# A fused attention kernel's gate split into two calendar steps, with a rearranged calendar

## The reference

```python
# cross attention on 77 context rows, 16 heads of 32, keys masked by length
x = x + softmax(mask((LN(x) @ Wq) @ (ctx @ Wk).T / sqrt(32))) @ (ctx @ Wv) @ Wo

# self attention whose four projections are mixtures of low-rank experts
y = LN(x)
h = relu(mean(y, axis=tokens) @ gw1.T + gb1)          # the gate: one vector a sample
logits = h @ gw2.T + gb2                              # 8 experts
top_vals, top_idx = top_k(logits, 2)
gates = softmax(top_vals)
# for p in q, k, v, o:
#   p(y) = y @ Wm.T + sum_k gates[k] * ((y @ V[idx_k].T) * S[idx_k]) @ U[idx_k].T + b
x = x + o(softmax(q(y) * scale @ k(y).T) @ v(y))
```

## Time and profile before

| | us |
|---|---|
| median of 3 runs | 1512.65 |
| lowest and highest | 1509.66, 1518.13 |
| the profiled execution | 1515.14 |
| its span, first to last instruction | 1513.4 |

### The profile page before, as it was taken

The page is one execution under the profiler, slowest core; times in us unless marked ns, Lnnn a source line. Parts: engine busy times, 40 slices in busy tenths (PEclk is TensorE's granted clock), DMA queues, the critical chain, the costliest instruction groups (busy, mean ns, idle before and its releaser), DMA issues.

```text
span 1513.4 us, 17021 instructions
## 1 busy us (share of the span) xinstructions
PE 1415.1 (94%) x5624; PEld 704.1 (47%) x5624; DVE 987.9 (65%) x1719; ACT 860.1 (57%) x1491; POOL 680.9 (45%) x411
## 2 busy tenths in 40 slices
PE   4998999899989999899989999899989999899877
PEld 3534444455444454445444454455445444444332
DVE  4363577776777677776777677776777676665552
ACT  1425374866467664766557664776557664655441
POOL 2011125454645354454545354354545354556553
PEclk9878999999999999999999999999999999899977
DMA  5423322522324322622334222522234221521220
GB/s 203 111 94 103 78 57 74 153 68 61 99 80 107 80 54 81 165 60 71 81 98 106 76 58 78 157 71 71 75 104 105 75 60 50 154 56 36 56 61 28
DMA packets 78238, 130.80 MB, mean 86 GB/s; under 512 B 26358, under 2 KB 31094, under 8 KB 75079
## 3 DMA queue, kind: packets, MB, share of 16 engines
q1 hardware_dynamic: 74055, 128.66, 31.9%
q10 hardware_dynamic: 4096, 1.06, 0.3%
HBM read 66.08 MB, written 12.21 MB: 52 GB/s over the span
## 4 chain that ended last, share of the span: by engine, by line
PE 82%; ACT 5%; DMA 4%; DVE 4%; SPq 3%; issue 2%; POOL 1%; ACTq 0%; POOLq 0%; DVEq 0%
PE pj L1090 40%; PE sc L1147 8%; PE acc L1204 8%; PE scT L1175 8%; PE sc L1136 3%; PE pj L1084 2%; PE scT L1168 2%; PE pj L1192 2%; PE pj L1120 2%; PE pj L1184 2%; DMA qsc<-qsc 2%; PE pj L1213 2%; ACT probs L816 2%; SPq L581 1%; PE pj L1076 1%
## 5 line engine op out<-in xcount | busy, mean ns | idle before, releaser
L816 ACT ACTIVATE probs<-scT 128x512 f32<-128x512 f32 x512 | 290.4, 594 | 320.2 <-PE scT L1175 317.8
L928 DVE TENSOR_REDUCE negmax<-sc 128x1 f32<-128x512 f32 x512 | 338.3, 684 | 156.7 <-PE sc L1147 155.2
L1147 PE MATMUL sc<-ks,qs 96*128 96x512 f32 x512 | 295.0, 599 | 35.5 <-DVE negmax L928 27.6
L679 POOL TENSOR_TENSOR probs_sum<-probs_sum,probs 128x1024 f32<-128x1024 f32 x128 | 300.7, 2366 | 58.1 <-ACT probs L816 57.6
L955 DVE RECIPROCAL inv_sum<-pj 128x128 f32<-128x128 f32 x256 | 224.1, 920 | 63.3 <-PE pj L1192 27.9
L1175 PE MATMUL scT<-qs,ks 99*128 99x512 f32 x512 | 250.6, 523 | 8.6 <-ACT probs L816 4.5
L1090 PE MATMUL pj<-XT,Wqk 128*128 128x512 f32 x512 | 257.7, 605 | 0.3 <-DVE Wqk L1027 0.2
L675 POOL TENSOR_TENSOR probs_sum<-probs 128x1024 f32<-128x1024 f32 x64 | 150.8, 2369 | 179.8 <-ACT probs L816 179.7
L685 POOL TENSOR_TENSOR uv_stack<-UVS_sb,uv_stack 96x1024 fp32r<-96x1024 f32 x32 | 75.6, 2361 | 246.9 <-ACT UVS_sb L723 246.9
L1147 PEld LDWEIGHTS sc<-ks,qs 96*128 96x128 f32 x512 | 100.6, 198 | 141.0 <-issue 75.0
L1175 PEld LDWEIGHTS scT<-qs,ks 99*128 99x128 f32 x512 | 98.4, 196 | 128.7 <-ACT probs L816 61.4
(11 more groups left out here) (102 smaller groups left out, 1753.7 us busy)
## 6 DMA issues: line engine op xcount, KB each, us to landing
Wqk<-in_WmT SPq DMA_DIRECT2D x16, 1024.0 KB, 5.9
Wvo<-in_WmT SPq DMA_DIRECT2D x16, 1024.0 KB, 7.5
UVS_sb<-in_UVS SPq DMA_DIRECT2D x64, 192.8 KB, 3.5
qs<-stage_lo SPq DMA_DIRECT2D x136, 64.0 KB, 2.1
qs<-qs SPq DMA_DIRECT2D x34, 256.0 KB, 3.0
X<-in_x SPq DMA_DIRECT2D x8, 1024.0 KB, 5.3
ks<-stage_lo SPq DMA_DIRECT2D x128, 64.0 KB, 2.0
ks<-ks SPq DMA_DIRECT2D x32, 256.0 KB, 3.0
```

Source lines behind the costliest of these rows:

```text
L679: nc.gpsimd.tensor_tensor(probs_sum[:, pair], probs_sum[:, pair], probs[:, kt % 2, pair], ALU.add)\
L816: nc.scalar.activation(probs[:, kt % 2, jj, :], scT[:, ST[step], :], ACT.Exp, scale=SCALE)\
L928: nc.vector.tensor_reduce(negmax[:, 0, n:n + 1], sc[:, SC[step], :], AX.X, ALU.max, negate=True)\
L1147: nc.tensor.matmul(sc[:, SC[step], :], qs[0:3 * DH, slot, jj, t * P:(t + 1) * P], ks[0:3 * DH, slot, jj, :], start=True, stop=True).then_i ...
```

## The change

The gate's handler on DVE is cut in two calendar steps. `gate_top` keeps the logits, the maxima and the indices. The new step `gate_scale` comes later in the calendar and has a part on ACT and one on DVE. ACT takes the exponential of the difference of the two logits directly, with the second as bias and the first scaled by -1, and then by an affine activation adds the two row patterns with the exponential as factor. DVE adds one, inverts, and multiplies the signs with both results in one operation. `pick` waits for the whole of the shorter `gate_top`, `uv_hi` for `gate_scale`.

```diff
@@ increments
     if kind == "gate_top":
-        return {"pj_full": 1, "pj_left_by_dve": 1, "gate_step": 9, "gate_exp": 1}
+        return {"pj_full": 1, "pj_left_by_dve": 1, "gate_step": 2}
+    if kind == "gate_scale":
+        return {"gate_exp": 2, "gate_step": 3}
@@ ScalarE
-            def gate_top(step, b):
-                act.wait_ge("gate_step", act.after("gate_step", *step, k=3))
-                nc.scalar.activation(g[:, 1:2], g[:, 0:1], ACT.Exp).then_inc(sems["gate_exp"], 1)
+            def gate_scale(step, b):
+                act.wait_ge("gate_step", max(act.after("gate_step", "gate_top", b), act.after("gate_step", "gate_scale", b - 1)))
+                nc.scalar.activation(g[:, 0:1], top[:, 0:1], ACT.Exp, bias=top[:, 1:2], scale=-1.0)\
+                    .then_inc(sems["gate_exp"], 1)
+                act.wait_ge("gate_exp", act.after("gate_exp", *step, k=1))
+                nc.scalar.activation(g[:, 1:2], stack_rows_sb[:, 1:2], ACT.Identity, bias=stack_rows_sb[:, 0:1],
+                                     scale=g[:, 0:1]).then_inc(sems["gate_exp"], 1)
@@ VectorE, gate_top
-                step_done(nc.vector.max_index(top_at[:, b % 2, :], top[:], logits[:]))
-                step_done(nc.vector.tensor_tensor(g[:, 0:1], top[:, 1:2], top[:, 0:1], ALU.subtract))
-
+                nc.vector.max_index(top_at[:, b % 2, :], top[:], logits[:]).then_inc(sems["gate_step"], 1)
+
+            def gate_scale(step, b):
                 dve.wait_ge("gate_exp", dve.after("gate_exp", *step))
-                step_done(nc.vector.tensor_scalar(g[:, 2:3], g[:, 1:2], 1.0, None, ALU.add))
-                step_done(nc.vector.reciprocal(g[:, 3:4], g[:, 2:3]))
-                step_done(nc.vector.tensor_tensor(g[:, 4:5], g[:, 3:4], g[:, 1:2], ALU.mult))
-
-                step_done(nc.vector.tensor_tensor(g[:, 5:7], stack_rows_sb[:, 0:2], g[:, 3:5], ALU.mult))
-                step_done(nc.vector.tensor_tensor(g[:, 7:8], g[:, 5:6], g[:, 6:7], ALU.add))
-                step_done(nc.vector.tensor_scalar(gate_signed[:, b % 2, :], stack_rows_sb[:, 2:4], g[:, 7:8], None,
-                                                  ALU.mult))
+                nc.vector.tensor_scalar(g[:, 2:3], g[:, 0:1], 1.0, None, ALU.add).then_inc(sems["gate_step"], 1)
+                dve.wait_ge("gate_step", dve.after("gate_step", *step, k=1))
+                nc.vector.reciprocal(g[:, 3:4], g[:, 2:3]).then_inc(sems["gate_step"], 1)
+                dve.wait_ge("gate_step", dve.after("gate_step", *step, k=2))
+                if b >= 2:
+                    dve.wait_ge("uv_scaled", dve.after("uv_scaled", "uv_hi", b - 2, OP))
+                nc.vector.tensor_scalar(gate_signed[:, b % 2, :], stack_rows_sb[:, 2:4], g[:, 1:2], g[:, 3:4],
+                                        ALU.mult, ALU.mult).then_inc(sems["gate_step"], 1)
```

All other changes are numbers: every entry of `CALENDAR` and `OWN` has new times, the period stays. Most move a step past a few neighbours. The ones that the next part speaks of:

```diff
 CALENDAR
-    "context": (-1662,),
+    "context": (-2070,),
-    "gate_top": (224,),
+    "gate_top": (235,),
+    "gate_scale": (349,),
-    "uv_hi": (359, 435, 610, 2992),
+    "uv_hi": (368, 514, 614, 3004),
 OWN
-    "context_keys": {(0, 0): -3752, (0, 1): -3229, (1, 0): -3140, (1, 1): -3087, (2, 0): -3021, (2, 1): -2917,
-        (3, 0): -2789, (3, 1): -2140},
-    "context_values": {(0,): -4865, (1,): -943, (2,): 108, (3,): 229, (4,): 361},
+    "context_keys": {(0, 0): -7883, (0, 1): -3570, (1, 0): -3359, (1, 1): -3340, (2, 0): -3280, (2, 1): -2935,
+        (3, 0): -2399, (3, 1): -1750},
+    "context_values": {(0,): -2137, (1,): -1089, (2,): 61, (3,): 221, (4,): 371},
```

More of the change, by code:

```diff
@@ new lines @@
+    "wm_load": {(7, 3): 20464, (0, 0): -185, (0, 1): -287, (0, 2): 597},
+    "uv_load": {(7, 3): 15834, (0, 0): 322, (0, 1): 354, (0, 2): 475},
+    "uv_hi": {(7, 3): 20376, (0, 0): 354, (0, 1): 473, (0, 2): 584},
+    "uv_lo": {(7, 3): 25932, (0, 0): 404, (0, 1): 491, (0, 2): 627},
+    "weff": {(7, 3, 0): 31424, (7, 3, 1): 32766, (7, 3, 2): 36119, (7, 3, 3): 39486, (0, 0, 0): 422, (0, 0, 1): 441,
[6 rows of a table added]
+    "load": {(0,): -7488},
+    "stats": {(0, 0): -5406, (0, 1): -5343, (0, 2): -4845, (0, 3): -4369},
@@ L161 @@
+    "token_sums": {(0, 0): 148, (0, 1): 157, (0, 2): 194, (0, 3): 196},
+    "gate_hidden": {(0,): 227},
+    "gate_top": {(0,): 245},
+    "gate_scale": {(0,): 288},
+    "pick": {(0,): 311},
 }
@@ L177 @@
            "cdivide": QUOTIENTS, "out1": product(FOUR, FOUR), "residual1": product(FOUR), "residual_bias": [()],
-           "token_sums": product(FOUR), "gate_hidden": [()], "gate_top": [()], "uv_hi": product(FOUR), "uv_lo": product(FOUR),
+           "token_sums": product(FOUR), "gate_hidden": [()], "gate_top": [()], "gate_scale": [()], "uv_hi": product(FOUR), "uv_lo": product(FOUR),
            "weff": product(FOUR, FOUR), "qk": product(JOBS, PAIR, FOUR), "qk_split": product(JOBS, PAIR),
@@ L603, in pick @@
             def pick(step, b):
[L604 removed]
+                sp.wait_ge("gate_step", sp.after("gate_step", "gate_top", b))
                 chosen[b] = [queue.value_load(top_at[0:1, b % 2, k:k + 1], min_val=0, max_val=E - 1) for k in range(2)]
@@ L708, in uv_hi @@
                 act.wait_ge("weights_loaded", 16 * 9)
-                act.wait_ge("gate_step", act.after("gate_step", "gate_top", b))
+                act.wait_ge("gate_step", act.after("gate_step", "gate_scale", b))
                 act.wait_ge(f"uv_loaded{n}", act.after(f"uv_loaded{n}", "uv_load", b, p))
@@ L990, in gate_top @@
             def gate_top(step, b):
-                n = 0
-                def step_done(ins):
-                    nonlocal n
-                    n += 1
-                    ins.then_inc(sems["gate_step"], 1)
-                    wait = settle if n == 1 else dve.wait_ge
-                    wait("gate_step", dve.after("gate_step", *step, k=n))
                 dve.wait_ge("pj_full", dve.after("pj_full", *step))
@@ L1003, in gate_top @@
                 settle("pj_left_by_dve", dve.after("pj_left_by_dve", *step))
-                step_done(nc.vector.max(top[:], logits[:]))
+                dve.wait_ge("gate_exp", dve.after("gate_exp", "gate_scale", b - 1))
+                nc.vector.max(top[:], logits[:]).then_inc(sems["gate_step"], 1)
+                settle("gate_step", dve.after("gate_step", *step, k=1))
                 if b >= 2:
```

150 lines of the change are left out of this document (69 added, 81 removed), and 54 rows, old and new, of tables (CALENDAR, OWN).

## The result

The changed kernel takes 1458.18 us in the median of four runs (1454.26 to 1459.78), the kernel before, beside it, 1511.55 (1509.66 to 1518.13). The ratio is 0.9636, with a 95% interval of 0.9606 to 0.9667.

A forecast was written before the change was run, and what follows sets the result against it. TensorE was taken to set the pace. Terms of 25.2 (gates), 3 (qsc), 5.6 (start), 1.5 (gate 0) and 2 (last sample) sum to 37.3 us: 1515.14 becomes 1477.8, median-adjusted to 1475; range 1460 to 1498.

The forecast's parts named there:

- For the rest I take nothing: Remaining calendar moves, with no price in the trace: 0 us, plus or minus 6 us (1 us a sample).
- the `qsc` term: TensorE's waits for the stack qsc: loading the next sample's keys earlier saves 3 of 4.7 us.
- six gates: Gate stall in six of eight samples: idle 4.2 to 1.5 us, plus 1.5 of clock; 4.2 each, 25.2 us.
- start to gate 0: Kernel start: with context_keys first, TensorE begins 5.6 us earlier, all of it gained; bounds 3 and 7.
- gate 0 to gate 1: Gate of sample 0: normalize comes first, so of TensorE's 1.97 us wait for xhat 1.5 us go.
- gate 7 to the end: Last sample: TensorE's 3.8 us of waits for shift DMAs lose 2 us in the new order.
- the port rival: Scalar operations of gate_scale block behind GpSimd in two-port mode, losing 1 to 2 us a sample: 1486, chance 0.03.
- in sample 7 GpSimd is not adding: Gate of sample 7: no stall there, one reason why only six of the eight gates have it.
- The low clock after the stall: The 4 us after the gate's stall run at clock 0.57, costing 1.5 us a gate; expected to vanish.
- What is late next: After the gate, ACT's transpose copies leave about 1.0 us idle, the second operand's stack 0.5: 1.5 us in all.
- that path came 0.5 us late once already ..., and I take 0.5 again: Stack of the second operand after the gate, some 6 us behind the row copies: 0.5 us of idle a sample.
- more than the sum: Rival: stall, qsc and shift waits all go, first cross attention closes up; 56 us, 1457, chance 0.11.

The follow-up runs named there:

- e1: Kernel before with the split gate in the old calendar, gate_scale put ahead of the first uv_hi; 1487.26 us, ratio 0.9823.
- e7: e1 with two moves added, the first context values later and context ahead; 1470.21 us, ratio 0.9705.
- e5: Kernel before with the first sample's context values placed behind the fourth key block, and their load moved; 1503.88 us, ratio 0.9932.
- e3: Kernel before, gate not split, its four two-tensor DVE operations written with the second input as a per-partition scalar; 1489.48 us, ratio 0.9835.
- e4: Kernel after with gate_scale moved right behind gate_top, where GpSimd is adding; 1471.78 us, ratio 0.9721.
- e9: Kernel after with context back at its old distance from the output stores; 1465.14 us, ratio 0.9659.
- the second profile of the kernel after: Kernel after, unchanged, run once more: 1458.55 us, ratio 0.9613; the profiled execution took 1466.22 us.
- e6: Kernel before with context ahead, so the next sample's keys load some 33 us earlier; 1508.89 us, ratio 0.9949.
- e8: Kernel after with the OWN (first sample's own times) of before and e1's entry for gate_scale; 1466.17 us, ratio 0.9671.
- e11: Kernel after with the OWN of e7, differing from e7 in CALENDAR alone; 1457.09 us, ratio 0.9619.
- e10: Kernel after with the gate_scale of sample 0 alone right behind its gate_top; 1456.21 us, ratio 0.9614.
- e2: Kernel before's one-block gate in the new CALENDAR and OWN; 1510.56 us, ratio 0.9972.

## Why the prediction was right and where it was wrong

The step that failed is "For the rest I take nothing": it gave 8.7 us in the six samples and 4.3 us in the last part. The gates were under-sized besides, and the `qsc` term was priced by its waits alone, without the lower clock behind them. The table splits the difference of the spans by terms. The gate is e1's gain between gates 1 and 7, the context what e7 has beyond e1 there, the rest what the kernel after has beyond e7:

```
us                         forecast (bounds)   measured   from
six gates                  25.2 (6 to 34)      28.3       1024.79 -> 996.46, e1
qsc waits                   3   (0 to 4.7)      6.7       996.46 -> 989.73, e7
rest of the order, 6 x      0   (-6 to 6)       8.7       989.73 -> 981.04, after
start to gate 0             5.6 (3 to 7)        7.7       e5 alone: 5.7
gate 0 to gate 1            1.5 (0 to 2)        0.0
gate 7 to the end           2                   6.6       e7 has 2.3 of it
sum                        37.3                58.0
```

The three terms of the six samples carry the chance of single executions: e1's has its one sample of 169.95 us. By the median sample (170.76, 165.50, 165.01 and 163.44 us) times six they are 31.6, 2.9 and 9.4.

**What stalled.** Right. Two-input DVE operations behind GpSimd's additions: e3 shows it with only the form of four operations changed. That L1018 and the scalar operations were never slow in the kernel before held as read; e3 and e4 show that the two-element ones can be, the port rival at 0.03 being right on the blocking and not on the price here, as `gate_scale` lies where GpSimd is idle. One reading was wrong: "in sample 7 GpSimd is not adding". It adds until 1299.92, and L1010 and L1015 take 0.93 and 1.46 us there; only L1017 comes after it. TensorE still has no long wait there (0.6 us for `negmax` at most), so the count of six stands.

**The low clock after the stall.** Right that it goes with the stall: 0.57 became 1.00, and TensorE's busy time of a sample fell by 1.2 us in e1's first four samples (164.9 to 163.7), against 1.5 forecast (3.66 x 0.43 is 1.6). But the same loss follows a late `qsc` stack, as e1, e9 and the second profile of the kernel after show, and the forecast has no term for that.

**What is late next.** The right engine and tile, over-sized. I let ACT be 1.0 us late and the stack of the second operand 0.5; measured were 0.67 and nothing, and in e1 0.5 and 0.3. So a gate gave 5.3 us in e1's median sample, not 4.2. What was mis-sized is the step "that path came 0.5 us late once already ..., and I take 0.5 again": one late transfer in six samples was charged to all six, and ACT's 1.0 was too much as well.

**The cost of the added operations.** The two activations took 295 and 387 ns, 0.68 us together where I took 0.6 with their semaphores. DVE stands 1.20 us for them, twice the forecast, and TensorE waits for none of it, as forecast: no reciprocal or `shift` appears among the waits after.

**The context.** The wait went almost whole (1.1 us left in e6, 0.8 in e7, nothing in the first profile of the kernel after, one of 1.7 us in the second) where I took 3 of 4.7. The 6.7 us of e7 over e1 is more than the waits give (5.0 - 0.8 = 4.2): the wait of 2.8 us in e1's long sample brought the lower clock with it, so that sample is 4.5 us over the median of the six. By the median sample the term is 2.9 us, about the 3 forecast; e9, which takes the move back, has 1 us a sample and 7 us more in one. So the move is worth 3 to 7 us here, most of it by whether such a wait occurs.

**The rest of the calendar.** Here the prediction failed most: "For the rest I take nothing, with plus or minus 6 us." It gave 8.7 us in the six samples, and 4.3 in the last part. e7, e8, e11 and after agree on the first: samples of 165.0 us with the old `CALENDAR`, 163.4 to 163.6 with the new one. 7.7 of the 8.7 us are TensorE's busy time, which fell from 984.46 to 976.73, and 1.0 its idle time. In two of e7's samples, of 165.12 and 164.97 us of busy time, the clock is low for a while right after the gate, here from 586 on:

```profile
586.00:590.00 4.00, 3.97 (x8) 1.78 (x8) 1.24 (x8) 3.90 (x7) 3.92 (x4) 0.57 0.06 9
```

The other four have 163.5 to 163.8 us, and the six of the kernel after 162.7 to 162.9, all at 1.00. So some 3 us of the 7.7 are the clock, and some 5, 0.8 us a sample, are the same matmuls closer together at full clock. The largest change in a group of matmuls is that of the scores (over the six samples, e7 and after: busy us, mean ns, idle before):

```profile
L1148 PE MATMUL sc<-ks,qs 96*128 96x512 f32 x384 | 216.6, 587 | 0.8
```

```profile
L1148 PE MATMUL sc<-ks,qs 96*128 96x512 f32 x384 | 195.4, 542 | 0.0
```

That doesn't show that they waited in e7. Single ones take about 0.4 or about 0.8 us in the timelines of both, the modelled ends of neighbours overlap, and other groups went up in the new order (L1169 from 544 to 598 ns in the mean, L1121 from 450 to 478), so that 21 us less in this group are under 8 in all. The prediction took all of TensorE's busy time as fixed work, and 0.8 us a sample of it was not. Which of the many moved steps does it was not tried apart and stays open.

**The start.** TensorE's first matmul came at 13.70 (13.5 forecast), and e5 gives 5.7 for it alone, the forecast's 5.6. In the new calendar it is 7.7, and e7 with the old calendar has 7.3 already; where these 2 us over e5 come from is not shown.

**Gate 0.** The 1.5 us came with the split gate in the old calendar (e1: no wait for `xhat`, 142.87 us, 2.4 less) and did not come in the new one. There the wait for `xhat` turned into two for `XT`, 1.46 us together. e10 is 2.9 us shorter in this stretch and e7, at 139.03, 6.2. Most of it is no wait: TensorE is busy 137.47 us at a clock of 0.91 in the kernel after, 133.62 at 0.94 in e10 and 131.73 at 0.96 in e7. What lowers the clock here was not tried apart.

**The last part.** 3.8 us of shift waits were to lose 2; they lost 0.9. The waits for the stacks `ks` and `qs` went from 3.7 and 3.0 us to 1.8 and 1.1, those for ACT's `probs` and GpSimd's `probs_sum` rose from 2.9 and 2.6 us to 5.0 and 4.4, and TensorE's busy time fell by 3.9 (188.11 to 184.21). The new calendar with the old gate (e2) ends as late as before, 219.1, and the new gate in the old calendar (e1) too, 220.6, so it takes both; why, I did not try.

**The sum.** 20.7 us were missed: 3.1 at the gates, 3.7 at `qsc`, 8.7 in the rest of the order, 2.1 at the start, 4.6 at the end, less 1.5 at gate 0. All but the rest and the end lie within or just outside their bounds; nearly every term was taken from the careful side, and all but gate 0 erred one way. The rival "more than the sum", 1457 at 0.11, came within 1.2 us, in part by luck: it has larger gates than measured, 4 us for the first sample's cross attention that no run shows apart, and nothing for the rest of the order. Its far half was left out of the range; it should have been in.

## What to carry to other kernels

Tiny DVE operations whose durations vary by a factor of ten, and end when a GpSimd operation ends, are a stall: give their second tensor input the form of a scalar operand, put them on ACT, or put them where GpSimd is idle. Here four rewritten lines (e3) gave about as much as the new gate with both engines. A calendar is fitted to the durations it was made with: the new one alone gave 0.3%, with the shorter gate it gave 2% beyond it, so try such parts together before giving one up. Price a wait of the busiest engine with what the clock costs behind it, and read a profile sample by sample: one sample that is 4 to 7 us over its neighbours, with one late transfer in it, can be a matter of that execution and not of the variant. And busy time of TensorE is not fixed work: another order of the same matmuls took 0.8 us a sample off it.

## What the runs showed of the hardware

- A DVE operation with two SBUF tensor inputs on one element a partition, 160 ns alone, took up to 1741 ns, and one on two elements up to 2277 ns, in each timeline shown to the end of a GpSimd addition of 2.37 us. A reciprocal (162 to 166 ns) and a one-element `tensor_scalar` (153 to 155) beside the same additions never did. Nor did a `tensor_tensor` of eight elements with one input in PSUM (`pj`) and one in SBUF, which in seven of the eight gates of the kernel before starts while an addition runs:

```profile
L1001 DVE TENSOR_TENSOR logits<-pj,gb_sb x8: 167/167/168, 125.0 to 1295.9; 128x8 f32<-128x8 f32 x8
```

- A two-element `tensor_scalar` did take longer (2123 ns for 288 in e4, 672 for 231 in e3), which the kernel before could not show.
- Operations with more per-partition scalar operands took longer: on DVE 153, 214 and 273 ns with none, one and two of them (L1013, L1010 and L1018 of e3), on ACT 203, 295 and 387 ns (L836 before, L840 and L843 after).
- The lower clock followed TensorE's stall of 4.2 us (0.57), and also single waits for `qsc` of 1.7 us (0.53 over 11 us) and 2.8 us (0.61 over 4 us). Idle times of 0.67 us at the gates of the kernel after left it at 1.00, but in two samples of e7 it fell (0.57 over 4 us) though no wait of TensorE in them reached 1 us.
